# Pairing the expert-row sums of the first layers on TensorE

## The reference

```python
sx, ix = top_k(sim[0], 8); sy, iy = top_k(sim[1], 8)     # 4 heads, 128 keys each side
scores, pk = top_k(all sums of pairs, 8)
down, up = down_embed[indices], up_embed[indices]        # 4096 experts x 256
w = silu(einsum('btd,bthkd->bthk', h, down)) * softmax(scores)
experts = einsum('bthk,bthkd->btd', w, up)
mlp = (silu(h @ Wg.T) * (h @ Wu.T)) @ Wd.T
return mlp + experts
```

## Time and profile before

| what | us |
|---|---|
| median of 3 runs | 3476.87 (3475.12 to 3482.71) |
| the profiled execution, its own time | 3483.59 |
| span of the profiled execution | 3481.7 |
| PE busy | 3287.7 (94%) |
| DVE busy | 2690.0 (77%) |
| ACT busy | 2114.0 (61%) |
| POOL busy | 2249.9 (65%) |

### The profile page before, as it was taken

The page is one execution under the profiler, slowest core; times in us unless marked ns, Lnnn a source line. Parts: engine busy times, 40 slices in busy tenths (PEclk is TensorE's granted clock), DMA queues, the critical chain, the costliest instruction groups (busy, mean ns, idle before and its releaser), DMA issues.

```text
span 3481.7 us, 102040 instructions
## 1 busy us (share of the span) xinstructions
PE 3287.7 (94%) x38106; PEld 2270.1 (65%) x38106; DVE 2690.0 (77%) x8770; ACT 2114.0 (61%) x6700; POOL 2249.9 (65%) x2083
## 2 busy tenths in 40 slices
PE   8899999886789999999999999999999999999998
PEld 6566766563446666666666666666666666666667
DVE  3688878774498888888887878888888788888873
ACT  4455555453266666666666766666766666666663
POOL 1677777676387667667666667667667667667650
PEclk9799999897899999999999999999999999999999
DMA  4677777778165565665665556565565555665552
GB/s 139 163 189 189 186 179 181 179 186 223 59 188 157 141 180 162 169 162 156 174 163 159 153 157 183 153 183 138 148 195 162 162 157 153 171 182 163 142 151 67
DMA packets 460045, 565.96 MB, mean 163 GB/s; under 512 B 51456, under 2 KB 396320, under 8 KB 458016
## 3 DMA queue, kind: packets, MB, share of 16 engines
q1 hardware_dynamic: 418448, 425.06, 44.2%
q0 software_dynamic: 40960, 134.25, 15.9%
q10 hardware_dynamic: 144, 0.13, 0.0%
HBM read 368.26 MB, written 178.45 MB: 157 GB/s over the span
## 4 chain that ended last, share of the span: by engine, by line
PE 69%; issue 2%; DVE 2%; POOL 0%; DMA 0%; ACT 0%; SPq 0%; DVEq 0%; POOLq 0%; ACTq 0%
PE pj L1875 28%; PE pj L1948 13%; PE y_ps L1931 9%; PE y_ps L1957 7%; PE o_ps L1906 6%; PE sc L1891 4%; PE tp L1853 1%; DVE l_probs L2159 0%; DVE l_qk_sin L2119 0%; DVE l_qk_cos L2117 0%; DMA l_qkT<-parked_qk 0%; DVE l_ss L2110 0%; DMA l_qk_gain<-in_gains 0%; DVE l_qk_turned L2143 0%; DVE l_p_turned L2176 0%
## 5 line engine op out<-in xcount | busy, mean ns | idle before, releaser
L1875 PE MATMUL pj<-w_qkv,l_xT 128*128 128x512 f32 x2304 | 1084.9, 608 | 13.5 <-ACT l_qk_sq L1997 10.7
L1816 POOL TENSOR_TENSOR l_qk_rot<-l_qk_cos,l_qk_sin 128x512 f32<-128x512 f32 x376 | 547.4, 1456 | 626.6 <-DVE l_qk_sin L2119 626.1
L1875 PEld LDWEIGHTS pj<-w_qkv,l_xT 128*128 128x128 f32 x2304 | 419.7, 192 | 431.7 <-issue 396.7
L511 POOL DMA_INDIRECT f_rows<-in_emb,f_expert x512 | 505.6, 987 | 225.6 <-issue 142.4
L2006 ACT ACTIVATE l_probs<-l_probs,l_low 128x96 f32<-128x96 f32 x1536 | 553.2, 367 | 5.0 <-DVE l_low L2159 4.4
L2159 DVE CUSTOM_DVE_ANT_0 l_probs<-sc,l_shut,l_r_q 128x96 f32<-128x96 f32 x1536 | 385.0, 308 | 208.6 <-PE sc L1891 208.3
L1948 PE MATMUL pj<-l_xnT,l_w 128*128 128x256 f32 x2112 | 481.1, 380 | 2.8 <-issue 2.8
L1948 PEld LDWEIGHTS pj<-l_xnT,l_w 128*128 128x128 f32 x2112 | 402.9, 191 | 96.4 <-issue 23.2
L1821 POOL TENSOR_TENSOR l_r_q<-l_ssm,l_minus_half 128x8 f32<-128x8 f32 x188 | 337.9, 1797 | 15.7
L1931 PE MATMUL y_ps<-w_o,l_oT 128*128 128x256 f32 x1536 | 339.6, 379 | 1.8 <-ACT l_oT L1978 1.8
L2119 DVE TENSOR_TENSOR l_qk_sin<-l_qk_raw,l_rope 128x512 f32<-128x512 f32 x384 | 337.5, 879 | 0.0
(11 more groups left out here) (328 smaller groups left out, 5750.4 us busy)
## 6 DMA issues: line engine op xcount, KB each, us to landing
parked_qk<-l_qk_turned SPq DMA_DIRECT2D x192, 512.0 KB, 3.0
l_qkT<-parked_qk SPq DMA_DIRECT2D x384, 256.0 KB, 5.4
parked_p<-l_p_turned SPq DMA_DIRECT2D x384, 192.0 KB, 2.4
l_pT<-parked_p SPq DMA_DIRECT2D x768, 96.0 KB, 2.7
w_qkv<-in_L_ffn_Wqkv SPq DMA_DIRECT2D x12, 1024.0 KB, 7.8
l_w<-in_ff_w SPq DMA_DIRECT2D x6, 1408.0 KB, 7.5
f_rows<-in_emb,f_expert POOLq DMA_INDIRECT x512
w_o<-in_L_ffn_Wo SPq DMA_DIRECT2D x6, 1024.0 KB
```

The costliest lines, as they stand in the source:

```text
L511: pool.indirect_dma_start(rows[:, j % RH, k, :], None, dram["emb"], bass.IndirectOffsetOnAxis(ap=expert[:, n % 2, at:at + 1], axis=0)).the ...
L1816: pool.tensor_tensor(qk_rot[:, i % ROTS, :], qk_cos[:, b, :], qk_sin[:, b, :], ALU.add).then_inc(rotated if s == 0 else pool_front, 1)
L1875: last = pe.matmul(pj[b][:, :], xT[:, k, t * P:(t + 1) * P], w_qkv[:, k, s * INNER + c * 512:s * INNER + (c + 1) * 512], start=(k == 0), s ...
```

## The change

Only `ORDER["tensor"]` is written anew. Without the `c_up` pieces the list is the same as before, and the `c_up` pieces keep their own order. Each even `c_up` is set directly ahead of the next odd one. The odd ones keep their places among the other pieces, except that `c_up15` already had `c_up14` one piece ahead and `c_up13` had `c_up12` directly ahead. The lists of the other engines, the buffers and all waits are unchanged. For one steady batch (batch 1):

```diff
-        a_o.3 c_y0.1 c_up0.1 d_hT.0 c_up1.1 d_k.0 d_q.0 a_y.3 d_v.0 d_s.0 b_gt.2 c_up2.1 b_m0.2 d_pT.0 b_m1.2 d_o.0 b_qa.2 b_qb.2 c_up3.1 b_m2.2
-        b_m3.2 c_up4.1 e_v.0 e_hT.0 b_h1.2 e_w.0 b_h0.2 e_q.0 c_up5.1 e_sa.0 c_up6.1 c_y1.1 c_up7.1 e_pT.0 e_o.0 c_up8.1 a_hT.4 c_hT.2 e_y.0 e_cT.1
-        e_u.0 c_q0.2 c_q1.2 c_up9.1 c_sa.2 b_cT.3 a_k.4 c_sb.2 c_up10.1 a_q.4 b_hT.3 e_k.1 a_v.4 c_up11.1 a_z.4 c_m0.2 c_m1.2 c_m2.2 c_m3.2 c_up12.1
-        c_up13.1 b_g.3 c_m4.2 c_m5.2 c_up14.1 c_m6.2 c_up15.1 c_m7.2 c_fold.1
+        c_y0.1 d_hT.0 c_up0.1 c_up1.1 d_k.0 d_q.0 a_y.3 d_v.0 d_s.0 b_gt.2 b_m0.2 d_pT.0 b_m1.2 d_o.0 b_qa.2 b_qb.2 c_up2.1 c_up3.1 b_m2.2 b_m3.2
+        e_v.0 e_hT.0 b_h1.2 e_w.0 b_h0.2 e_q.0 c_up4.1 c_up5.1 e_sa.0 c_y1.1 c_up6.1 c_up7.1 e_pT.0 e_o.0 a_hT.4 c_hT.2 e_y.0 e_cT.1 e_u.0 c_q0.2
+        c_q1.2 c_up8.1 c_up9.1 c_sa.2 b_cT.3 a_k.4 c_sb.2 a_q.4 b_hT.3 e_k.1 a_v.4 c_up10.1 c_up11.1 a_z.4 c_m0.2 c_m1.2 c_m2.2 c_m3.2 c_up12.1
+        c_up13.1 b_g.3 c_m4.2 c_m5.2 c_m6.2 c_up14.1 c_up15.1 c_m7.2 c_fold.1
```

## The result

The kernel before took 3479.79 us here (median of four runs, 3475.12 to 3484.0), the changed one 3575.51 us (3572.34 to 3579.7): slower, ratio 1.0271 (95% interval 1.0255 to 1.0287), 96 us. The forecast was 3529 in a range up to 3552. The side is right, the size about half.

What follows compares the result with a forecast made beforehand. PE taken as busiest, its waits set by a chain over DVE, ACT and POOL. Six steady batches 43 us, batch 0 3, batch 7 2, clock 4: 52 us, 3529 us forecast from the 3476.87 median; range 3492 to 3552.

Steps and rivals of the forecast that it cites:

- the mechanism and its two places: On POOL, e_rstd queues behind late c_gather6, b_root behind late c_gather8 and c_gather9; 4.0 and 2.9 us a batch.
- the clock term: Over the whole run, longer waits bring more PE work at the lower clock: 4 us, between 0 and 18.
- The two waits: Per steady batch, PE loses 4.0 us through late e_rstd and 2.9 through late b_root; with 0.33 net, 43 us in six.
- about where c_up3 started: In batch 2, the moved c_up2 starts near c_up3's old 324.31, taken as 323.9, so c_gather6 comes 5.1 us later.
- for my 5: Outside the six steady batches: 3 us (0 to 7) in batch 0 and 2 us (0 to 4) in batch 7.
- c_up0's place costs nothing: On PE, moving c_up0 is free, as c_gather4 came later than the new release anyway.
- 0.33 us a batch: On PE: c_up8 moved behind c_hT costs 0.86 us, pairing c_up10 and c_up14 saves 0.53; net loss a batch.
- PE idle ahead of e_hT and b_h1: Sign that the forecast is right: PE waits there for work delayed by late e_rstd; b_h1 4.0 us later.
- hidden to within half a microsecond: On ACT, c_diag reaches each c_up no earlier than its new place allows, to within that margin.
- what is hidden: Delays costing nothing: c_gather12 and c_gather14 3 to 4 us late, c_up0's and c_up6's moves, c_diag's waits.
- The savings of the joins: On PE, pairs of c_up save 0.16 to 0.37 us each, at most 1.59 us a batch, 12.7 in eight.
- the falling clock: Rival: a slow-clock stretch on PE behind every new wait, 18 us instead of 4; 66 us, 3543; 12%.

Runs made afterwards that it cites:

- ring of eight: Half rows gathered, eight ring places instead of four: old order 3462.26 us, changed order 3489.40, 27 us apart; with four places 99 us apart.
- two_sums_back: Changed kernel with c_up2 and c_up4 back in their old places, the other six joined: ratio 1.0068 to the kernel before, 24 us slower.
- diag_ring_3: Changed kernel with three buffers for the diagonals instead of two: ratio 1.0266 to the kernel before.
- roots_first: Changed kernel with e_rstd moved ahead of c_gather6 and b_root ahead of c_gather9 on POOL: ratio 1.0218 to the kernel before.
- free_joins: Kernel before with only c_up10 and c_up14 moved next to c_up11 and c_up15: ratio 1.0010, 3.5 us slower.
- only_up2: Kernel before with only c_up2 moved next to c_up3: ratio 1.0062, 22 us slower.
- filled_waits: Changed kernel with extra identity matmuls, results unread, ahead of TensorE's waits in steady batches: ratio 1.0214 to the kernel before.

## Why the prediction was half right

**Right: the mechanism and its two places.** c_gather6 behind c_up2 with e_rstd behind it, c_gather8 and c_gather9 with b_root behind them: POOL's rows show both, and a ring of eight, which takes these waits away and touches no order, takes 72 of 99 us. The pairs, x32 in 1.96 us, are as forecast.

**The step that failed: the clock term.** I took 4 us, bounds 0 to 18, "because a part of them lies where PE waits again". Reckoned as there, by half of PE's busy time at the lower clock, it is an estimated 33.5 us in the six steady batches with the ring of four and 27.5 with the ring of eight. Filling the waits returns about 20 and 29 us by the ratios, net of what the filling costs. The upper bound was wrong as well: I priced one slow stretch of 7 us a batch more. In every steady batch there is one of 6.8 us around e_v's wait, and that between c_up7 and c_up9 is 14 to 17 us long, where the kernel before has 3 to 14; batches 2 and 3 have a third.

**The two waits were priced about rightly.** Without the clock's 33.5 us the six batches lose 80.9 - 33.5 = 47.4 us, where I had 43. c_gather6 starts 1.90 to 1.98 us behind its pair's start (I had 1.91), and b_bias in batch 2 comes 379.31 - 365.82 = 13.49 us behind the pair of c_up4 (I had 13.6). The stretches between the pairs grow by more than I had, from c_up3 to c_up5 by 17.0 - 10.7 = 6.3 us in the mean of batches 1 to 6, since the work behind e_v's wait runs at half clock at first. I placed the pair "about where c_up3 started". It comes later, as c_up1 to c_up3 grows by 2.1 us in the same mean, in batches 2 and 3 most, where the slow stretch lies ahead of the pair. That moves the pair and does not lengthen the wait behind it: e_v waits for 4.15 and 5.89 us in batches 2 and 3, and for 4.41, 4.19 and 4.14 in batches 1, 4 and 5.

**Smaller misses.** Outside the six batches 92.6 - 80.9 = 11.7 us were lost, for my 5. "c_up0's place costs nothing" looked at its gather alone: c_up0 had stood between c_y0 and d_hT, and without it d_hT waits for a bank, 0.73 us in batch 2 and 1.57 in batch 4. That is a part of the 24 us that the six other joins cost in two_sums_back, where I had 0.33 us a batch; the shares of the rest are open.

**Wrong in a detail that did not set the size.** I expected PE idle ahead of e_hT and b_h1. It is e_v that waits, since b_qk holds its bank, so the wait could not be filled with e_v's 2.00 us. ACT's wait for c_ups, called hidden to within half a microsecond, reached 5.2 us, and without it (diag_ring_3) the time is the same within its interval.

**Incomplete: "what is hidden".** I followed each late gather to the root behind it and not to its own rows. In roots_first c_gather6 is just as late behind its pair, and without the roots in the way the time falls by 18 us only. The savings of the joins show in no run: free_joins, which has two of them and none of the two waits, is 3.5 us slower.

**Of the rivals**, the falling clock was the nearest (3543) and was also too low. Its 18 us for the clock compare with 33.5. Its rule, a slow stretch behind every new wait, holds for e_v's wait in all six batches and for d_pT's in two of five with 0.64 to 0.79 us. Why c_up2 and c_up4 cost more together (0.0203) than alone (0.0142) stays open. A part may be that only_up2 gets 1.7 us a batch back between c_up7 and c_up9, which the changed kernel does not.

## What to carry to other kernels

A consumer that is moved back behind its neighbour in a ring frees its place late, and the next producer then has two places to fill at once: follow the late rows, and not only what queues behind their issue. If TensorE gets a new wait of some 4 us, price the slow clock behind it as the normal case, at the busy time of the work that stands there. Of a piece that is moved, ask also which wait it had covered where it stood. To learn whether a wait or its place in a queue is the cause, enlarge the ring, if need be with smaller data: reordering the queue showed the next late thing and made another.

## What was not expected of the hardware

A wait of 0.79 us on TensorE, with small transposes and 4-row matmuls ahead of it, was followed by 6.5 us at half clock in batch 2, and one of 0.77 us likewise in batch 3; waits of 0.75, 0.64 and 0.64 us at the same place in batches 1, 4 and 5 were not. The same 16 matmuls of b_q take 2.93 us at half clock and 1.58 us at the full one, and e_v 3.75 and 2.00. The kernel before, batch 2:

```profile
322.80 1.58 PE L663 MATMUL fp<-f_hT_b,f_ctxT_b 64*128 64x256 f32 x16
...
328.49 2.00 PE L550 MATMUL fp<-f_e_wv,f_ctxT_e 128*128 128x256 f32 x8
```

The four transposes of c_hT, at the full clock before, went from 0.66 to 1.12 us. In filled_waits some 600 matmul records without any use, with which PE is busy for 53 us more in all, made the kernel 20 us shorter.
